# A new closing stage in a fused attention and mixture-of-experts kernel: residual and projection read during attention, the bias added on TensorE, and no separate blocks for semaphores

## What is computed

```python
# attention: 32 query heads of 16, 8 groups of keys and values, causal; ctx gives keys and values
attn = softmax(mask(q @ k.T / 4))
out = einsum(attn, v).reshape(B, S, D)          # (4, 512, 512)
x = x + tanh(g_xattn) * (out @ w_o.T + b_o)     # the closing stage: x1
# feed-forward on layernorm(x): router over 16 experts (top 4, two of four groups), shared experts
h = layernorm(x)                                # x2
scores = softmax(h @ Wg.T)                      # logits from Wg
y = sum over chosen experts of combine * (silu(h @ W1.T) * (h @ W3.T)) @ W2.T
z = (silu(h @ Ws1.T) * (h @ Ws3.T)) @ Ws2.T
x = x + tanh(g_ffn) * (y + z)
```

## Time and profile before

| | us |
|---|---|
| three runs | 1601.21, 1604.19, 1607.18 |
| median | 1604.19 |
| the profiled execution | 1603.01 |
| its span, first to last instruction | 1601.1 |

### The profile page before, as it was taken

One profiled execution on the slowest core, in us unless ns is written; L12 is line 12 of the kernel. 1 busy time (PEld: TensorE's weight loads), 2 busy tenths in 40 slices (PEclk: granted clock), 3 DMA queues, 4 the chain that ended last, 5 costly groups with the idle time before them and its releaser, 6 DMA issues. The chain is left out here.

```text
span 1601.1 us, 27965 instructions
## 1 busy us (share of the span) xinstructions
PE 1296.8 (81%) x8634; PEld 955.8 (60%) x8635; DVE 686.6 (43%) x1765; ACT 580.6 (36%) x1016; POOL 755.0 (47%) x812
## 2 busy tenths in 40 slices
PE   6566069999999465657999996999998999899996
PEld 3233046444444223345787775888888888788895
DVE  2112036888888223445774102134334333453300
ACT  2111004666666401113222222444443444344453
POOL 4111002333333202223434444888787887777785
PEclk9887579999999877767999997999999999999998
DMA  6344232333333345643201203455554555554543
GB/s 191 107 143 143 84 96 59 103 100 102 102 98 94 96 146 193 210 167 107 79 27 53 79 14 107 120 133 121 127 125 113 126 130 163 120 120 115 124 73 45
DMA packets 95099, 178.31 MB, mean 111 GB/s; under 512 B 26212, under 2 KB 27748, under 8 KB 94024
## 3 DMA queue, kind: packets, MB, share of 16 engines
q1 hardware_dynamic: 69800, 114.03, 22.4%
q0 software_dynamic: 23456, 59.31, 17.2%
q10 hardware_dynamic: 1792, 4.33, 0.8%
HBM read 113.29 MB, written 64.03 MB: 111 GB/s over the span
## 5 line engine op out<-in xcount | busy, mean ns | idle before, releaser
L460 DVE CUSTOM_DVE_ANT_0 a_mb<-a_mb,late 128x128 f32<-128x128 f32 (+3 forms) x512 | 244.5, 510 | 81.4 <-PE a_mb L495 73.9
L1257 DVE CAST e_w<-e_w 128x480 fp32r<-128x480 f32 x135 | 95.8, 719 | 411.8 <-DMA e_w<-in_w2T 411.8
L378 POOL TENSOR_SCALAR_AFFINE_SELECT a_at<-a_at 128x256 f32<-128x256 f32 x256 | 104.5, 408 | 286.2 <-ACT a_at L441 286.0
L441 ACT ACTIVATE a_at<-a_eb 128x1024 f32<-128x1024 f32 (+3 forms) x256 | 179.8, 705 | 130.7 <-PE a_eb L514 130.1
L1391 PE MATMUL e_gate<-e_w,e_xT 128*128 x948 | 189.1, 353 | 22.5 <-DVE e_w L1266 14.8
L1410 PE MATMUL e_yps<-e_w,e_hT 128*128 x711 | 189.2, 407 | 18.3 <-POOL e_hT L1296 17.3
L1391 PEld LDWEIGHTS e_gate<-e_w,e_xT 128*128 128x128 f32 x948 | 173.0, 209 | 39.1 <-issue 33.5
L1391 PE MATMUL e_up<-e_w,e_xT 128*128 x948 | 172.6, 331 | 0.0
L1287 POOL DMA_INDIRECT out<-e_y,scatter x79 | 130.5, 1652 | 55.2 <-DMA out<-e_y,scatter 41.7
L1410 PEld LDWEIGHTS e_yps<-e_w,e_hT 128*128 128x128 f32 x711 | 127.2, 189 | 48.6 <-POOL e_hT L1296 23.6
L1391 PEld LDWEIGHTS e_up<-e_w,e_xT 128*128 128x128 f32 x948 | 152.1, 191 | 0.0
(11 more groups left out here) (202 smaller groups left out, 1864.7 us busy)
## 6 DMA issues: line engine op xcount, KB each, us to landing
e_w<-in_w13T SPq DMA_DIRECT2D x16, 1408.0 KB
dq<-p_parts SPq DMA_DIRECT2D x48, 256.0 KB
a_q<-dq SPq DMA_DIRECT2D x64, 192.0 KB
do<-a_o SPq DMA_DIRECT2D x32, 256.0 KB, 2.1
dx<-c_x POOLq DMA_DIRECT2D x8, 1024.0 KB, 8.5
e_w<-in_w2T SPq DMA_DIRECT2D x16, 512.0 KB
a_k<-dk SPq DMA_DIRECT2D x64, 98.0 KB
p_ctx<-in_ctxT SPq DMA_DIRECT2D x4, 1024.0 KB, 5.2
```

The source lines that it names most:

```text
L378: eng.affine_select(out=square, in_=square, compare_op=ALU.is_ge, fill=0.0, base=0, pattern=[[0, 2], [1, P]], channel_multiplier=-1).then_ ...
L441: eng.activation(at[r % 2][:, ch, 2 * hp:2 * hp + 2, ch * P:SEQ], eb[hp][:, :, ch * P:SEQ], ACT.Exp, scale=0.25).then_inc(s_exp, 1)
L460: eng.tensor_tensor_reduce(out=b[:, 0:w], in0=b[:, 0:w], in1=io["late"][:, SEQ - w:SEQ], scale=1.0, scalar=3 * NEG, op0=ALU.add, op1=ALU.m ...
L1257: eng.tensor_copy(w[rows, r, cols], w[rows, r, SIDE + cols.start:SIDE + cols.stop].bitcast(F32)).then_inc(s_high, 1)
```

## The change

The closing stage is written anew, with parts of its work moved elsewhere:

- The buffer `e_w` is now made before the attention. During the first four and the last four attention steps SP reads into it `w_o` (4 pieces), `Wg`, the bias, and all of `x` (16 pieces of 128 tokens); the closing stage adds in place, and the shared stage reads `x1` from there. Stores and reads of `dx1`, and the stage's own reads of `x`, `w_o`, `Wg` and the bias, are gone.
- The reciprocals no longer go through memory: TensorE multiplies `c_inv` by a matrix of zeros and ones (`c_pick`, made by GpSimd with two selects) into PSUM (`c_den`), 16 matmuls. VectorE normalises `c_o` in place.
- The bias is split in three bfloat16 parts (7 VectorE instructions) and added by one bfloat16 matmul ahead of each tile's projection.
- `c_o`, `c_x2` and `c_x2T` have two buffers, `c_op` three. The loop is written out, and TensorE's order is tile by tile.
- The weights of the shared experts are read on SP's queue, the first two through one buffer `c_wraw`.
- The first expert's weights are read ahead of the last sequence of the shared stage, since `x1` lies where they go.
- `inverse_deviation` has 11 VectorE instructions in place of 5, most of them of one column.
- `start` is gone: each engine raises the semaphores that it signals itself, at the head of the stage (`begin`). The constants are made in the projection stage.

The diff, cut to its core:

```diff
+def residual(io, b):
+    buf, at = (0, b * CH * D) if b < BATCH - 1 else (1, 2 * DOWN)
+    return io["w"][:, buf, at:at + CH * D].bitcast(F32).rearrange("p (j d) -> p j d", j=CH)
-def start(nc, sems):
-    with nc.Block(no_gpsimd_drain=True) as block:
-        @block.vector
-        def _(eng):
-            for sem in sems:
-                eng.sem_inc(sem, 1)
+def begin(eng, *made):
+    for sem in made:
+        eng.sem_inc(sem, 1)
...
# attention, SP, at the end of a step's body
+            def fetch(i, r, t):
+                if not isinstance(i, int):
+                    return
+                if i < NB:
+                    eng.dma_start(io["wo"][:, i, :], io["woT"][i * P:(i + 1) * P, :]).then_inc(io["s_wo"], 16)
+                if i == 0:
+                    eng.dma_start(io["wg"], io["wgT"].rearrange("(c p) n -> p c n", p=P)).then_inc(io["s_wo"], 16)
+                    eng.dma_start(io["bias"], io["bo"].broadcast_to([P, D])).then_inc(io["s_wo"], 16)
+                for n in (2 * r, 2 * r + 1) if i < NB else (2 * (NB + r), 2 * (NB + r) + 1):
+                    eng.dma_start(residual(io, n // CH)[:, n % CH], io["x"][n * P:(n + 1) * P, :]).then_inc(io["s_x"], 16)
...
# closing, SP
             eng.dma_start(sums[:], ...).then_inc(s_sums, 16)
             load_o(0)
+            load_o(1)
+            eng.dma_start(wraw[:]..., io["ws1T"]...).then_inc(s_ws[0], 16)
+            eng.wait_ge(s_op, CH + 1)
+            load_o(2)
+            ... (ws2T into its place)
+            eng.wait_ge(s_wlow, KD + 1)
+            eng.dma_start(wraw[:]..., io["ws3T"]...).then_inc(s_ws[1], 16)
+            eng.wait_ge(s_op, 2 * CH + 1)
+            load_o(3)
...
# closing, GpSimd
             for b in range(BATCH):
-                (stores of x1, x2, x2T, with a wait for each)
+                store(b)                      # x2, then x2T; two buffers each
                 if b < 3:
                     low_weights(b)
...
# closing, VectorE
+            for b in range(BATCH):
+                for j in range(CH):
+                    i = b * CH + j
+                    eng.wait_ge(s_op, i + 2)
+                    eng.scalar_tensor_tensor(out=x1[b][:, j], in0=op[i % RING][:], scalar=tg[:, 0:1], in1=x1[b][:, j], ...)
+                    eng.wait_ge(s_x1, i + 2)
+                    eng.bn_stats(stats[:, j, :], x1[b][:, j]).then_inc(s_st, 1)
+                    if b + 1 < BATCH:
+                        normalise(b + 1, j)
...
# closing, TensorE
+            def widen(b, k):
+                d = b * KD + k
+                if d >= 2:
+                    eng.wait_ge(s_on, d)
+                eng.matmul(den[k % 2][:], pick[:, d * P:(d + 1) * P], inv[:], start=True, stop=True).then_inc(s_den, 1)
+            def project(b, j):
+                i = b * CH + j
+                eng.wait_ge(s_on, (b + 1) * KD + 1)
+                if i >= RING:
+                    eng.wait_ge(s_x1, i - RING + 2)
+                eng.matmul(op[i % RING][:], three[:], triple[:], start=True, stop=False)
+                for k in range(KD):
+                    mm = eng.matmul(op[i % RING][:], o[b % 2][:, k, j * P:(j + 1) * P], wo[:, k, :], start=False, stop=k == KD - 1)
+                mm.then_inc(s_op, 1)
...
+            for b in range(BATCH):
+                for j in range(CH):
+                    project(b, j)
+                    if b + 1 < BATCH:
+                        widen(b + 1, j)
+                    if b:
+                        turn(b - 1, j)
+                        if j:
+                            score(b - 1, j - 1)
+                if b:
+                    score(b - 1, CH - 1)
...
# shared, SP
-            load_expert(eng, io, 0, 0)
             for b in range(BATCH):
-                if b:
+                if b == BATCH - 1:
                     eng.wait_ge(io["s_base"], 16 * CH * b)
-                eng.dma_start(x1, dram["x1"]...).then_inc(s_x1, 16)
+                    load_expert(eng, io, 0, 0)
```

More of the change, by code:

```diff
@@ new lines, in stage_close @@
+        s_x2out, s_xTout = [dsem(f"c_sx2out{i}") for i in range(2)], [dsem(f"c_sxTout{i}") for i in range(2)]
+        s_tg, s_eps, s_one, s_above, s_pick, s_rec, s_three, s_split, s_triple = (
+            sem(f"c_s{n}") for n in ("tg", "eps", "one", "above", "pick", "rec", "three", "split", "triple"))
+        s_den, s_on, s_op, s_x1, s_st, s_mv, s_root, s_newton, s_x2 = (
+            sem(f"c_s{n}") for n in ("den", "on", "op", "x1", "st", "mv", "root", "newton", "x2"))
+        s_tr, s_xT, s_lg, s_lc, s_whigh, s_wlow = (sem(f"c_s{n}") for n in ("tr", "xT", "lg", "lc", "whigh", "wlow"))
@@ L1325, in _ @@
         def _(eng):
+            begin(eng, s_upc, s_xT, s_act, s_hT, s_y)
             def part_x(g, r):
```

378 lines of the change are left out of this document (177 added, 201 removed).

## The result

The changed kernel took 1564.36 us (median of four runs, 1558.31 to 1569.32) against 1605.68 for the kernel before (four runs): a ratio of 0.9745, 95% interval 0.9704 to 0.9787. The prediction was 1548.0 with a range of 1537 to 1565. So the direction and the range held, the range by 0.6 us only (two of the four runs lie above 1565), and the point was 16 us too low. The profiled execution took 1565.75, span 1563.8.

What follows compares the result with a forecast made beforehand. No engine bounds the closing stage, a chain of waits does (VectorE 79.0 us for `c_den`). Gains 45.4 (stage) + 5.0 (front) + 3.6 (boundaries) + 1.5 (shared read) - 0.5 (attention reads) = 55.0, from 1603.0 to 1548; range 1537 to 1565.

Steps and rivals of the forecast that it cites:

- last projection, P: Closing stage: the last sequence's last projection is done 104.6 us after the stage's first transfer, S.
- tail: Closing stage, from the last projection to the next stage's start: 24.0 us, partly at half clock.
- The rival that the change would be slower: Closing stage: TensorE's clock stays at 0.50 between short waits, 90 us more, 1638; chance 0.02.
- The bias preparation: Head of the closing stage: VectorE's five casts and two subtractions ahead of the reciprocal, 4.3 us with gaps.
- Rival 2: Closing stage: bias casts wait for GpSimd's `c_pick` writes, later inverse deviations held too; 3 to 4 us more, 1552; chance 0.10.
- The stalls for `x2`: Closing stage: TensorE waits for `x2` 0.8 us in sequence 2 and 1.4 in sequence 3.
- The tiles between: Closing stage, TensorE's work per tile: 4.56 us projection with bias and widening, 0.55 transposes, 1.12 logits.
- The last `c_o`: Closing stage: this read, queued behind the third weight's, lands at S + 73.9 and stalls TensorE 1.8 us.
- Boundaries: Between stages: one block fewer saves 1.2 us each at projection-attention, attention-closing and shared-experts, 3.6 us, bounds 0 to 5.
- the one that they cost nothing: Stage boundaries: they cost the same without `start`, so 3.6 and half of the front's 5 are lost, 1554; chance 0.05.
- The front: Kernel start: without the constants' block the first transfer leaves at about 1.0 instead of 6.29; gain 5.0 us.
- The rival by which they delay the rows of maxima: Attention: the moved reads delay 8 steps by up to 2 us each, 1564; chance 0.04.

Runs made afterwards that it cites:

- run with gaps: The changed kernel, with each of GpSimd's weight subtractions waiting for the semaphore of the one before it: 1561.75 us, closing stage 138.0.

## Why the prediction was right, and by how much it was off

By its own steps, in the closing stage of the first trace:

| step | predicted | measured |
|---|---|---|
| reciprocal ends | S + 7.7 | S + 12.3 |
| first projection | S + 12.5 | S + 18.7 |
| a tile of sequence 1 | 6.2 | 5.1, then 5.8 |
| last projection, P | S + 104.6 | S + 117.5 |
| tail | 24.0 | 25.0 |
| stage | 128.6 | 142.5 |

- **The mechanism was right.** The round trip of the reciprocals was what the stage waited for (79.0 us for `c_den`), and without it TensorE is busy 111.4 of 142.5 us. What isn't shown is how the gain of 31.5 us divides: no run puts the round trip back by itself, or takes away the second buffers or the order tile by tile. The rival that the change would be slower needed a clock stuck at 0.50; it was 1.00 under the steady matmuls.
- **The bias preparation was mis-sized: 4.3 us, and it was 9.0 to the reciprocal's start.** Rival 2 had this mechanism with a start at S + 6.5 to 7. Two held instructions cost 1.7 and 1.6 us, the start of VectorE's list 1.0, the memsets ahead of the casts 0.9, and casts and subtractions were 0.5 longer by themselves. The gaps, for which the sum had left 1.1, came to almost nothing (0.03 to 0.04 each). With the reciprocal ahead of it the first projection is at S + 14.0.
- **From the reciprocal to the first projection 4.8 was 6.4**, since TensorE had been idle for 4.7 us before the widening, its clock was at 0.72 from 552 to 558, and its four matmuls took 5.37 us with their waits.
- **The stalls for `x2`, taken as 0.8 and 1.4, were 4.3 and 5.1.** This is the step that failed most. The prediction allowed up to 3 us more where GpSimd works, reading as one instruction's worth (1.19). The runs showed that the whole run of four to six instructions is waited for, 5.7 to 6.5 us. Each wait brought the clock down, which cost another 1.3 and 0.9 us at the next tile. Rival 2 named the later inverse deviations as well, but its price of 3 to 4 us in all was a fifth of what GpSimd's list cost; the order of that list alone was worth 20.0 us. The prediction also said that the lock speaks against the change at one place, the bias casts; the dearer place was the inverse deviation beside the split weights.
- **The tiles between were priced too high.** Transposes were taken as 0.55 a tile and logits as 1.12; in the steady tile of 5.76 us they took 0.44 and 0.81. This hid part of the stalls.
- **The Trainium skill** (SBUF — State Buffer, SBUF: two separate sides) speaks of the shared port as a lock held for a whole instruction. The run with gaps agrees with it (0.90 to the end of the subtraction under way), and the changed kernel, where instructions follow back to back, shows more than it says: 5.80 for four of them. The measurement decides.
- **The last `c_o`** was to land at S + 73.9 and stall TensorE 1.8 us. It was waited for until S + 83.3 and stalled 1.79. The agreement is partly luck: both sides were late, the read because GpSimd's run had been placed 4.8 us too early (its subtractions end at 607.99, S + 68.2, not 63.4) and because `c_o` took 15 us behind the third weight's issue, not 10.5; TensorE because of the steps above. In the kernel with gaps, where TensorE waited less for `x2` ahead of it, the same read cost 7.67.
- **The tail was nearly right as a sum, 24.0 against 25.0.** Its parts were off in both directions: the first transpose at + 11.6 instead of + 7.6 (the held instruction again), and the rest shorter: 8.1 us from there to the last store's issue instead of 10.0, and 5.3 from that to the next stage instead of 6.4.
- **Boundaries were under-priced.** The four that were taken away gave 1.2, 2.2, 2.7 and 1.5 us, 7.7 in all and not 4.8. Of the rivals, the one that they cost nothing is out. The attention's gain of 2.2 us is this boundary: from its last store to the next transfer it was 4.53 and is 2.33.
- **The front** gave 5.3 us and the boundary behind the stage 1.2, but the two together with the stage gained 5.0: the projections' stage took back 1.5 in this trace, where 0.3 was foreseen. A stage that differs by 9 us between executions can't tell that.
- **The reads during the attention** cost nothing that can be seen, as forecast. The rival by which they delay the rows of maxima gave 1564, which is the time that came out, and yet it is wrong: the attention did not grow (330.0 with them, 329.4 without). A time that fits is no evidence for a mechanism; the stages' lengths are.
- **The shared stage** gained 3.0 (2.7 predicted with its boundary). **The experts' stage** was 4.4 us longer in the trace; that it varies is shown, why it does was not looked into.

## What to carry to other kernels

Look at what GpSimd has queued back to back when a short VectorE instruction on the critical chain is due: the price can be the whole queue (5.7 to 6.5 us here; one instruction in the kernel before), and the cure that cost nothing here was to place that queue elsewhere in its own list, beside work that reads PSUM. When a wait is taken away and the time doesn't move, look for the wait that stood in parallel, and price an edit only together with it. A block between stages has a price of its own, and a few idle matmuls ahead of a serial tail can be cheap (2.84 us of them, in a wait, took 3.0 us off this one).

## What the runs showed of the hardware

- **Which forms are held.** Beside GpSimd's float32 subtractions, these VectorE instructions, of four or more columns and from and to SBUF alone, were held: the addition on 128x4 (5.80), the product of two such (5.75), the multiplication and addition on 128x4 (4.55), `x2` on 128x512 (four in 5.18 instead of 1.92). Not held were one-column forms (four in 0.34), the reciprocal of 128x4 (0.18), the statistics of 128x512 (0.69), which also stay in SBUF, and the normalisation and residual, which take an operand from PSUM (0.67, 0.75). Beside the selects a cast (2.10 instead of 0.43) and a subtraction (2.26 instead of 0.69) of 128x512 were held and the reciprocal of 128x512 was not (3.35). So the number of columns and SBUF alone don't decide it. In the kernel before the normalisation had both operands in SBUF and took 1.50.
- **How long.** To the end of GpSimd's run if its instructions follow back to back (5.7 to 6.5 us for four to six), to the end of the one under way if each waits for the one before it (0.90; the cast between the two selects).
- **What stays open.** In the kernel before, GpSimd's instructions followed back to back as well (five in 6.14 us), and yet the held ones took 1.19 each, one GpSimd instruction at a time. The form of the VectorE instruction doesn't explain it, since the same form was held 5.75 us in the changed kernel. What does was not found.
- **A block between stages** with 10, 16 and 24 raised semaphores costs 1.7, 2.2 and 2.6 us (4.94 against 2.33 from last store to first transfer for the last).
